# Attention slots of a four-layer graph network: a third query product between a chunk's keys and its scores; in the last layer, last subtractions and exponentials ahead of additions and value copies

## The reference

```
# third layer
q, k, v = x @ Wq.T, x @ Wk.T, x @ Wv.T + bv          # split into 12 heads
a = q @ k.T * 384 ** -0.5 + adj
o = softmax(a) @ v                                    # rows that are all zero give zero
x = layernorm(x + o @ Wo.T + bo)
# last layer
q, k, v = x @ Wq + bq, x @ Wk + bk, x @ Wv + bv
s = q @ k.T / sqrt(32) + beta * adj
s = where(adj > 0, s, -9e15)
x = layernorm(x + softmax(s) @ v)
```

## Time and profile before

| | us |
|---|---|
| median of 3 runs (2743.5 to 2744.87) | 2744.46 |
| the profiled execution's own time | 2737.55 |
| its span in the trace | 2735.8 |
| TensorE busy | 2505.6 (92%) |
| VectorE busy | 1982.6 (72%) |
| GpSimd busy | 1674.7 (61%) |
| ScalarE busy | 1288.8 (47%) |

### The profile page before, as it was taken

How to read it: one execution, slowest core, us unless ns; L and a number is a source line. 1 busy time by engine, 2 the same in 40 slices (tenths; PEclk the granted TensorE clock), 3 DMA queues, 4 the chain that set the end, 5 groups by cost and what they waited for, 6 DMA issues and landing times.

```text
span 2735.8 us, 57977 instructions
## 1 busy us (share of the span) xinstructions
PE 2505.6 (92%) x22272; PEld 2167.7 (79%) x22272; DVE 1982.6 (72%) x4101; ACT 1288.8 (47%) x2641; POOL 1674.7 (61%) x1700
## 2 busy tenths in 40 slices
PE   8999999999998999999999978999999988888885
PEld 7999999999986888888888857788777776666664
DVE  5788888888886766676666568778887765565554
ACT  2344344444433444434443445555555555555554
POOL 6756755755767766666666656555555555555554
PEclk9999999999999999999999989999999999999998
DMA  5011111221142222222222154444444444445443
GB/s 158 31 49 60 58 53 53 70 65 41 56 119 88 69 59 65 64 70 53 65 70 59 39 143 115 111 100 110 110 117 120 120 107 125 119 123 127 120 109 93
DMA packets 377188, 238.28 MB, mean 87 GB/s; under 512 B 201168, under 2 KB 374864, under 8 KB 376912
## 3 DMA queue, kind: packets, MB, share of 16 engines
q1 hardware_dynamic: 376912, 234.58, 32.2%
HBM read 133.84 MB, written 50.33 MB: 67 GB/s over the span
## 4 chain that ended last, share of the span: by engine, by line
PE 67%; issue 11%; POOL 10%; DVE 8%; ACT 3%; DMA 0%; SPq 0%; POOLq 0%; DVEq 0%; ACTq 0%
PE bank L344 14%; PE bank L1462 12%; PE bank L888 11%; PE pair L888 11%; PE bank L326 3%; PE pair L326 3%; PE pair L1492 2%; ACT h_keys L1593 2%; PE bank L359 2%; POOL h_logitsa L1857 2%; PE bank L874 2%; DVE h_rec L1745 2%; POOL h_logitsb L1857 2%; PE bank L912 1%; PE pair L912 1%
## 5 line engine op out<-in xcount | busy, mean ns | idle before, releaser
L1462 PE MATMUL bank<-h_hhia,whi 128*128 128x512 f32 x450 | 189.0, 420 | 33.4 <-ACT h_val L1610 23.7
L1610 ACT ACTIVATE h_val<-bank 64x192 f32<-64x192 f32 x512 | 169.3, 331 | 86.5 <-PE bank L1470 80.2
L1185 POOL TENSOR_TENSOR l_hlo<-l_hf,l_hhi 128x576 fp32r<-128x576 f32 x96 | 134.8, 1430 | 115.1 <-ACT l_hhi L1005 115.1
L1593 ACT ACTIVATE h_keys<-bank,h_keycol,h_halves 128x512 f32<-128x512 f32 x192 | 139.0, 775 | 134.1 <-PE bank L1462 134.1
L1857 POOL TENSOR_TENSOR h_logitsb<-h_logitsb,h_mx 128x256 f32<-128x256 f32 x192 | 113.6, 616 | 140.9 <-DVE h_mx L1723 138.7
L1492 PE MATMUL pair<-h_keys,h_q 64*64 64x128 f32 x3072 | 107.0, 277 | 101.0 <-ACT h_keys L1593 98.2
L412 ACT ACTIVATE l_sides<-bank 128x512 f32<-128x512 f32 x192 | 113.1, 595 | 176.1 <-PE bank L344 176.1
L1857 POOL TENSOR_TENSOR h_logitsa<-h_logitsa,h_mx 128x256 f32<-128x256 f32 x192 | 114.6, 621 | 124.0 <-DVE h_mx L1723 121.8
L1492 PEld LDWEIGHTS pair<-h_keys,h_q 64*64 64x64 f32 x3072 | 83.7, 134 | 130.3 <-ACT h_keys L1593 124.4
L1462 PE MATMUL bank<-h_hhia,wlo 128*128 128x512 f32 x450 | 180.6, 401 | 0.0
L1082 DVE TENSOR_TENSOR l_val<-bank,l_vec 64x384 f32<-64x384 f32 x256 | 142.3, 556 | 40.2 <-PE bank L888 37.3
(11 more groups left out here) (267 smaller groups left out, 7937.8 us busy)
## 6 DMA issues: line engine op xcount, KB each, us to landing
h_strips<-x SPq DMA_DIRECT2D x128, 192.0 KB, 3.7
h_pieces<-h_logitsa SPq DMA_DIRECT2D x256, 96.0 KB, 2.2
h_pieces<-h_logitsb SPq DMA_DIRECT2D x256, 96.0 KB, 2.2
l_hf<-xt SPq DMA_DIRECT2D x16, 864.0 KB, 4.8
l_x<-x SPq DMA_DIRECT2D x32, 384.0 KB, 3.2
h_za<-x SPq DMA_DIRECT2D x16, 768.0 KB, 4.8
h_zb<-x SPq DMA_DIRECT2D x16, 768.0 KB, 5.1
l_x<-x SPq DMA_DIRECT2D x15, 768.0 KB, 4.6
```

The lines of the kernel that those rows point to most:

```text
L1185: nc.gpsimd.tensor_tensor(hlo[:, c, :], hf[:, c, :], hhi[:, c, :], ALU.subtract).then_inc(lo_done, 1)
L1462: mm = nc.tensor.matmul(ring[k % 2][:, :], ww[:, c, m * P:(m + 1) * P], hh, start=(c == 0 and j == 0), stop=(c == KC - 1 and j == 2))
L1593: ins = nc.scalar.activation(keys[:, turn, :, h, :], ring[1][:, :].rearrange("p (g j) -> p g j", j=S), ACT.Identity, scale=halves[:, h:h + 1],
L1610: ins = nc.scalar.activation(val[S * p:S * p + S, 2 * t + b, :, p, 0:HD], src[S * b:S * b + S, :, p, :], ACT.Copy)
```

## The change

It moves instructions within the hand-written orders; none is added or taken away but that GpSimd's low parts are written as two loops.

- TensorE and ScalarE, every slot: the query product of chunk 1 (k = 2) comes before S0, that of chunk 2 (k = 4) before S1. ScalarE copies in the same order, with `final_apply` now behind the third copy.
- GpSimd, last layer from slot 17: one chunk of the low parts, then the subtractions of units 4 and 5, then the other two chunks, then `outputs_in`. Before: three chunks, `outputs_in`, subtractions.
- ScalarE, last layer from slot 17: exponential 4 before the second value copy, exponential 5 before the third. Before: behind the second and the third.
- VectorE, last layer: `probs_turned` between the maxima of units 1 and 2 of the next slot, as in the third layer, and no longer behind those of unit 3.

```diff
--- before.py
+++ after.py
@@ -1558,13 +1558,12 @@
             if n + 1 == groups:
                 pe.wait_ge(sh.w_ready, 19)
             if more:
-                query_key(n + 1, 0)
-                query_key(n + 1, 1)
+                for k in range(3):
+                    query_key(n + 1, k)
                 chunk_scores(n + 1, 0)
-                query_key(n + 1, 2)
                 query_key(n + 1, 3)
+                query_key(n + 1, 4)
                 chunk_scores(n + 1, 1)
-                query_key(n + 1, 4)
                 query_key(n + 1, 5)
         for t in range(T):
             output(slots - 1, t)
@@ -1648,18 +1647,21 @@
             if n:
                 exponential(n, 2)
                 exponential(n, 3)
-                if more and not alone:
-                    high_parts(n + 1)
+            if more and not alone:
+                high_parts(n + 1)
+            if n:
                 values_out(n, 0)
             if before:
                 outputs_high(n - 1, range(0, 2))
             if n:
+                if not before:
+                    exponential(n, 4)
                 values_out(n, 1)
-                exponential(n, 4)
+                exponential(n, 4 if before else 5)
             if before:
                 outputs_high(n - 1, range(2, 4))
             values_out(n, 2)
-            if n:
+            if before:
                 exponential(n, 5)
             values_out(n, 3)
             if more and alone:
@@ -1833,15 +1834,11 @@
             if more:
                 maxima(n + 1, 0)
                 maxima(n + 1, 1)
-            if project(n):
-                for t in range(T):
-                    probs_turned(n, t)
+            for t in range(T):
+                probs_turned(n, t)
             if more:
                 maxima(n + 1, 2)
                 maxima(n + 1, 3)
-            if not project(n):
-                for t in range(T):
-                    probs_turned(n, t)
         for t in range(T):
             divide(slots - 1, t)
         final_stats(slots - 1)
@@ -1858,8 +1855,8 @@
                                               .broadcast_to([P, 2, T, SQ]), ALU.subtract)
             ins.then_inc(sub_done, 1)
 
-        def low_parts(n):
-            for c in range(KC):
+        def low_parts(n, chunks=range(KC)):
+            for c in chunks:
                 pool.wait_ge(hi_done, KC * n + c + 1)
                 pool.wait_ge(lo_done, KC * n)
                 nc.gpsimd.tensor_tensor(hlo[n % 2][:, c, :], xt[n % 2][:, c, :], high(n)[:, c, :],
@@ -1895,15 +1892,19 @@
         take_off(0, 3)
         pool.wait_ge(vec_in, 16 * 3)
         for n in range(slots):
-            more, alone = n + 1 < slots, n <= groups
-            if n and more and not alone:
-                low_parts(n + 1)
-            if n:
+            before, more, alone = project(n - 1), n + 1 < slots, n <= groups
+            if more and not alone:
+                low_parts(n + 1, range(1))
+            if before:
                 outputs_in(n - 1)
             take_off(n, 4)
             take_off(n, 5)
             if n and more and alone:
                 low_parts(n + 1)
+            if more and not alone:
+                low_parts(n + 1, range(1, KC))
+            if n and not before:
+                outputs_in(n - 1)
             split_weights(sh, pool, "lo", *weights_of_slot(n))
             if n:
                 final_power(n - 1)
```

## The result

The changed kernel takes 2639.64 us (median of 4 runs, 2635.74 to 2640.42) where the kernel before, on the same chip, takes 2743.98 (4 runs, 2739.25 to 2744.87). The ratio is 0.962, with an interval of 0.9604 to 0.9637: faster by 104 us. The forecast was 2652, the range 2620 to 2684.

What follows compares the result with a forecast made beforehand. TensorE was taken as the bound, with regular idle gaps; in the last layer GpSimd's order caused the 3.4 us gap. Gains of 89 + 0 + 3 = 92 us against the median of 2744.46 gave 2652 us, range 2620 to 2684.

Steps and rivals of the forecast that it cites:

- The last layer, 89 forecast: Last layer: 14 slots shrink from 33.66 to 27.3 us, a gain of 89 us, with 72 and 104 for the bounds.
- the rival in which it still falls: Last layer: TensorE's clock still falls to 0.50 in each slot, 22 us come back, 2674 us; chance 0.08.
- score gaps: TensorE's idle stretches before S0 and S1, ended by ScalarE's key copy, 1.62 us each; a query product of 2.15 fills one.
- the loops meet: Last layer: three loops from slot to slot all end at 26 to 27 us; small waits add up, so 27.3.
- rival C: Last layer, set against the theory in the experiments: only one loop binds; no chance given.
- TensorE's loop: Last layer, TensorE and ScalarE: 25.7 us of products plus at most 1.3 for exponentials ahead of copies, 27.0 a slot.
- the pieces' loop: Last layer: load of probabilities 12.0 us, then transposes, maxima, divisions, subtraction and exponential: 25.7, up to about 1.4 more.
- the loop of VectorE and GpSimd: Last layer: from a slot's first maxima through subtraction, low parts, `outputs_in` and statistics to the next: 26.9 us, no idle time.
- The third layer, 0 forecast: Third layer: closed gaps win at most 0.5 us a slot, a VectorE-GpSimd collision offsets it; 0, 8 us either way.
- The passage and the tail, 3 forecast: Slot 16 between the layers gains 2 us; in the last slot the exponential starts one value copy sooner, 1 us.
- The slower rival: Last layer: pieces load in over 20.0 us, VectorE and then TensorE wait; 55 us slower, 2799 us; chance 0.02.

Runs made afterwards that it cites:

- relief for VectorE and GpSimd: The changed kernel with two of three low parts of the last layer moved from GpSimd to VectorE, behind its maxima of unit 5: 2640.46 us.
- the experiment with the pieces held back: The changed kernel with the next slot's mask transfers issued after the exponentials and ahead of the pieces on SyncE's queue, last layer: 2677.81 us.
- The two experiments on this layer: Absolute-maxima reductions left out: changed kernel 2596.16 us, kernel before 2732.63. Multiply's reciprocal input in PSUM: changed kernel 2600.59, kernel before 2732.16.
- two halves: Kernel before with only the new query product order: 2670.41 us. Changed kernel with the old product order, keeping the last layer's other new orders: 2681.93 us.
- one part alone: Early transposes on VectorE added to the kernel before with the new query product order, GpSimd's subtractions and ScalarE's exponentials as before: 2718.43 us.
- the first experiment: The kernel before with only the new order of query products on TensorE and ScalarE, in both layers: 2670.41 us, 0.9743.

## Why the prediction was right, and where it was off

**The last layer, 89 forecast, 92.5 measured.** The slot was put at 27.3 us and is 27.05. The two gaps closed as said, 3.40 to 0.19 and the score gaps to at most 0.4, and the clock stayed in full, so the rival in which it still falls is out. That the loops meet is what the rows read: TensorE is busy for 96% of the window (215.76 of 225), VectorE runs from the statistics to the transposes with 0.16 us idle. Two of the loops are seen to bind by turns. In the ten slots in which VectorE waits for the pieces, theirs does: it had no room when 2.64 us were put in, and relief for VectorE and GpSimd won nothing. In the other four slots VectorE doesn't wait for them, and in the one shown the work passes between VectorE and GpSimd without a break from one slot's first maxima to the next: 2399.95 to 2426.72, 26.77 us, where I had put 26.9. So rival C, one loop alone, falls, though by little: the waits for the pieces come to some 0.4 us a slot, and the slots without one took 26.4 to 26.9. A kernel with a shorter pieces' loop, which would confirm this, was not tried, and where TensorE's loop stands is not shown.

One term was too small: the pieces' loop, put at 25.7 us with up to 1.4 more. I took 12.0 us for the load from the last slot, the only one of that layer in which VectorE waited for it. In the experiment with the pieces held back VectorE waits for it in every slot, and it takes 12.05 to 13.83 us up to its use, 12.7 on the mean; why it varies stays open. And exponential 5 waits about 0.8 for a value copy: GpSimd's subtractions ended at 2413.22 + 2.51 = 2415.73, and it began at 2416.55. So the loop's length is about 27, the upper end of what I gave. That the slot came out within 0.3 us was partly luck: the loop of VectorE and GpSimd was right, but the 0.4 that I had added for loops that meet is covered by one of them, the pieces', which I had put too short.

**The third layer, 0 forecast, 2.5 measured over twelve slots.** Right, for the reasons given: the wait before the divisions is gone, the transposes wait for `h_o` (2.3 us a slot; I said 3), and the first division now falls on GpSimd's subtraction. VectorE and GpSimd in one slot, as in the earlier trace rows:

```profile
1969.81 0.55 DVE L1746 SCALAR_TENSOR_TENSOR h_rec<-h_amxb,h_rec 128x12 f32<-128x12 f32 x1
...
1969.71 1.19 POOL L1854 TENSOR_TENSOR h_logitsa<-h_logitsa,h_mx 128x256 f32<-128x256 f32 x2 [0.73 <-DVE h_mx L1724]
```

The first multiply takes 0.55 us where it took 0.18: 0.37 lost of the 0.5 that the slot could win, and 0.2 is what was won. The bounds (half a microsecond either way) had the sign open; it fell on the side of the gain. The two experiments on this layer show what could not be read before: VectorE's work is the bound there, and the multiply's collisions are some 2.5 us of each slot.

**The passage and the tail, 3 forecast, 6.3 measured.** The passage gave 2.6 (2 forecast). The tail gave 3.7 where I had counted one value copy (1 us). Of the 3.7, 3.18 lie between S0 and S2 of that slot (2681.28 to 2696.53 before, 2587.77 to 2599.84 now): one product has moved from behind S0 to ahead of it, and the gap before S1 fell from 1.54 to 0.36. I had counted only the earlier exponential, so this term was too small.

**The sum.** 92 forecast against the profiled execution's own time, 97 measured. By the medians it is 104, and the further 7 are the distance of before's profiled execution from its median; why it ran that much faster stays open. That S0 of slot 2 came 4.25 us later, most of it from layers without any edit, is open too; in the other kernels it moved by as much.

**The slower rival** (pieces late, TensorE after them) was given 0.02 with transfers slower than the trace shows. Late pieces come about without slower transfers, as the kernel with early transposes and the old GpSimd order shows: VectorE waited for them in ten of 14 slots. But of its 48 us they are only a part. In the four slots without such a wait it lost 2.2 us each as well, on a way that I had not listed: the transposes hold up the maxima of units 2 and 3, those the high parts, and the last subtractions stand behind the low parts made from them. The change moves the transposes and these subtractions together.

## What to carry to other kernels

In a loop in which engines pass work around, the parts of a change of order don't add: here two halves won 71 and 60 us and together 104, and one part alone made the kernel 48 us slower than without it. So sum each loop from one instruction back to the same instruction a slot later, transfers included, and change the orders that stand on the same loop together. Where an engine's gaps close and the time doesn't move, look for small instructions that run far above their shortest duration; here a 12-element multiply was worth more than the product order of its layer.

## What the hardware showed that I had not expected

- A 128 x 12 multiply with both inputs in SBUF took 930 ns beside GpSimd's additions, and 174 with one input in PSUM. It works the other way round as well: four GpSimd subtractions took 3.33 us beside VectorE's low parts (two SBUF inputs), 2.51 without.
- The granted clock fell to 0.50 behind gaps of 3.4 us and 3.95 us in the last layer, and stayed at 1.00 with a gap of 1.35 in the same place. It wasn't so in each slot: two of the 14 slots of the kernel before took 32.3 us, as at full clock, with a gap of 3.40 in the one shown. I had expected it to fall in the first experiment too.
- Sixteen transfers of 96 KB each, off the critical chain before, became a bound by their issue and landing, 12.05 to 13.83 us up to their use, while the mean share of busy DMA engines in the last layer is 0.59.
